# First attention and feed-forward of a two-layer block as one stage

## The chip, the cores and the metric

The kernel runs on one core of a Trainium2 chip. Such a core has TensorE (PE, matrix products and transposes), VectorE (DVE), ScalarE (ACT), GpSimd (POOL) and SyncE (SP, which here only issues DMAs). Each works through its own list of instructions in order, and they wait for each other by semaphores. The metric is the time of one execution on the device, in microseconds; lower is better.

## The reference

Four residual blocks on 2048 tokens of 256 values (8 sequences of 256), each followed by a layer norm. The change touches the first two:

```python
x = _layernorm(x + _L0_attn_ref(x, w_qkv, w_out, ln_scale, ln_bias))
x = _layernorm(x + _L0_ffn_ref(x, w_gate, w_up, w_down))
...
# attention, 16 heads of 16 values: q and k are rotated (rope), then normalised per head
a = jnp.einsum('bhnd,bhmd->bhnm', q, k) ** 4     # causal: the upper triangle is 0
out = einsum('bhnm,bhmd->bhnd', a / sum(a), v) @ w_out
# feed-forward, 1024 hidden values
return (silu(x @ w_gate.T) * (x @ w_up.T)) @ w_down.T
```

Then come a second attention (32 heads of 8, softmax with a bias) and a mixture of 8 experts with a shared one.

## The kernel before

Every matrix product with weights is done with operands split into a rounded high part and a rest: `product3` adds high x high, high x low and low x high, lines 415 to 417, so each product is three matmuls. ACT or POOL writes the high part, DVE or POOL the low one.

The kernel has four stages in order: first attention (`phase0`), first feed-forward (`feed_forward`), second attention (`phase2`) and the experts (`moe`). Every engine's code calls one function for each.

**First attention.** Eight batches of 256 tokens. A batch is worked off in eight slots, `p` = 0 to 7, each with two heads. In a slot PE does `scores` (lines 693 and 694, into banks 2 (p mod 2) and the next), ACT squares them out of PSUM (line 1258), POOL sets the upper triangle to zero (`affine_select`, line 2132, two instructions a slot), and the second squaring (`quartic`) falls to DVE in even slots (line 1661) and to ACT in odd ones (line 1241). In every second slot PE mixes four heads with v (`mix`, line 714). Between these each slot has a share of what the next batches need: `x_turn` (transpose x), `qk`, `v`, rotation and norm of the heads on DVE (`rope_half`, `centre`, `variance`, `normalised`, `times_scale`, `plus_bias`, `lo_parts`), their high parts on ACT (`hi_parts`, line 1228), `heads` (transposes, line 639), and of what the last batch needs: `c_turn`, `ct_turn`, `project`, `add`, `statistics`, `norm`. The tables `PE0` and `ACT0` say in which slot each stands. The one square root of a batch on ACT is `deviation` (line 1219). Middle batches run in a loop (`passes`).

POOL also splits the weights of the feed-forward: one unit of 128 x 768 a batch, in four pieces of 192 columns, a cast (line 2089) and a subtraction (line 2094) after each mask pair.

A finished batch is stored to `x1` in memory.

**First feed-forward.** Four passes of 512 tokens, each read back from `x1`. A pass has eight tiles of 128 hidden values: `gate_up` (12 matmuls of 512 columns, gate and up in two banks, two pairs of banks in turn), `silu` on ACT (line 1360), `product` on DVE (line 1814), `hidden_hi` on ACT, `hidden_lo` on DVE (line 1819), and two tiles later `down` (12 matmuls of 256 columns). The last pass has the start of the second attention between its tiles (`start_attention`).

## Time and profile before

| | |
|---|---|
| Median of three runs | 1083.01 us (1082.18 to 1087.15) |
| Profiled execution, its own time | 1081.15 us |
| Its span, first to last instruction | 1079.4 us |
| Mean granted PE clock | 0.945 |
| PE busy | 895.1 us, 83% |
| DVE busy | 701.5 us, 65% |
| ACT busy | 663.7 us, 61% |
| POOL busy | 292.6 us, 27% |

Busy shares are means over all stages. Matmuls are pipelined: a matmul's own length includes its way through the array, and the spacing of two starts is what one more costs. The clock is a share of full speed.

### The profile page before, as it was taken

The numbers are of one execution on the slowest core, as the hardware profiler recorded it, in microseconds if no ns is written. First come the engines' busy times: TensorE is split into PE (matmuls) and PEld (weight loads), VectorE is DVE, ScalarE is ACT, GpSimd is POOL, SyncE is SP. The second block draws the span as 40 slices with busy tenths as digits, with TensorE's granted clock in tenths as the row PEclk, the third lists the DMA queues.
The fourth block names the chain that finished last, engine by engine and source line by source line (L and its number), as shares of the span: only waits on it lengthen the run. The fifth ranks groups of instructions, "written<-read, shape, count | busy, mean of one in ns | idle before, by whom it ended". The sixth has DMA issues, their size and how long they took to land.

```text
span 1079.4 us, 21316 instructions
## 1 busy us (share of the span) xinstructions
PE 895.1 (83%) x6816; PEld 708.0 (66%) x6816; DVE 701.5 (65%) x2026; ACT 663.7 (61%) x1398; POOL 292.6 (27%) x417
## 2 busy tenths in 40 slices
PE   3577676766999998888888989898988899799993
PEld 2355555554888887566665656565655688698882
DVE  4767888883444455767788877888787654255445
ACT  2466667676232233888888878888888533256643
POOL 0255555455010110200202020202020226534436
PEclk9778989898899999999999999999999999999997
DMA  3001100112233310200101010111010402234443
GB/s 104 1 26 44 41 20 26 44 35 75 77 110 118 108 50 1 70 2 25 38 23 36 23 36 23 36 23 50 1 52 2 130 21 81 92 99 114 113 154 124
DMA packets 64868, 60.67 MB, mean 56 GB/s; under 512 B 18113, under 2 KB 60353, under 8 KB 64802
## 3 DMA queue, kind: packets, MB, share of 16 engines
q1 hardware_dynamic: 61394, 50.48, 16.0%
q0 software_dynamic: 3408, 9.34, 2.6%
q8 instruction: 38, 0.62, 0.3%
q14 instruction: 28, 0.23, 0.1%
HBM read 37.05 MB, written 22.75 MB: 55 GB/s over the span
## 4 chain that ended last, share of the span: by engine, by line
PE 50%; ACT 15%; DVE 14%; issue 11%; POOL 5%; DMA 2%; SPq 1%; DVEq 0%; ACTq 0%; POOLq 0%
PE ps L415 10%; PE ps L416 9%; PE ps L417 9%; ACT G L1310 6%; PE ps L821 6%; PE ps L639 4%; PE ps L838 3%; POOL xs L2216 3%; DVE G L1731 3%; PE ps L809 2%; ACT G L1320 2%; PE ps L714 2%; DVE RT L1652 1%; ACT G L1258 1%; ACT RT L1199 1%
## 5 line engine op out<-in xcount | busy, mean ns | idle before, releaser
L1310 ACT ACTIVATE G<-G,small 128x256 f32<-128x256 f32 x512 | 230.9, 506 | 54.7 <-DVE small L1731 53.3
L1731 DVE CUSTOM_DVE_ANT_0 G<-ps,nb 128x256 f32<-128x256 f32 x512 | 191.1, 419 | 74.9 <-PE ps L809 74.2
L821 PE MATMUL ps<-ident,G 128*128 128x128 f32 x1024 | 161.6, 288 | 39.9 <-ACT G L1310 38.0
L821 PEld LDWEIGHTS ps<-ident,G 128*128 128x128 f32 x1024 | 112.5, 143 | 76.3 <-issue 29.1
L2110 POOL TENSOR_SCALAR small<-small 128x2 f32<-128x2 f32 (+1 forms) x20 | 8.0, 400 | 461.7 <-DVE small L1535 461.7
L1320 ACT COPY G<-ps 128x512 f32<-128x512 f32 x192 | 111.3, 580 | 14.5 <-PE ps L821 14.1
L2132 POOL TENSOR_SCALAR_AFFINE_SELECT G<-G 128x256 f32<-128x256 f32 x128 | 75.7, 614 | 121.9 <-ACT G L1258 121.5
L639 PE MATMUL ps<-ident,RT 128*128 128x128 f32 x512 | 74.6, 293 | 20.2 <-DVE RT L1652 19.4
L415 PE MATMUL ps<-WU 128*128 128x512 f32 (+1 forms) x256 | 87.9, 343 | 1.5 <-DVE WU L1804 1.4
L416 PE MATMUL ps<-WU 128*128 128x512 f32 (+1 forms) x256 | 86.9, 340 | 0.0
L417 PE MATMUL ps<-WU 128*128 128x512 f32 (+1 forms) x256 | 86.6, 338 | 0.0
L639 PEld LDWEIGHTS ps<-ident,RT 128*128 128x128 f32 x512 | 61.3, 150 | 29.1 <-DVE RT L1652 15.7
L1360 ACT ACTIVATE G<-ps 128x512 f32<-128x512 f32 x32 | 19.1, 598 | 96.8 <-PE ps L417 96.8
L838 PE MATMUL ps<-G 128*32 128x256 f32 x1024 | 71.2, 397 | 0.8 <-ACT G L1320 0.8
L1814 DVE TENSOR_TENSOR G<-ps,G 128x512 f32<-128x512 f32 x32 | 22.1, 691 | 76.1 <-PE ps L417 76.1
L809 PE MATMUL ps<-RT 32*128 32x256 f32 x512 | 64.8, 331 | 6.8 <-DVE small L1731 2.8
L1258 ACT ACTIVATE G<-ps 128x768 f32<-128x768 f32 x64 | 52.1, 815 | 29.4 <-PE ps L694 28.2
L714 PE MATMUL ps<-ring,G 128*32 128x128 f32 (+1 forms) x512 | 32.5, 378 | 43.1 <-ACT G L1191 24.3
L809 PEld LDWEIGHTS ps<-RT 32*128 32x128 f32 x512 | 38.3, 184 | 42.0 <-issue 26.5
L415 PE MATMUL ps<-AW,RT 128*128 128x512 f32 (+1 forms) x128 | 54.2, 423 | 10.7 <-DVE nb L1707 4.4
L2094 POOL TENSOR_TENSOR WU<-wraw,WU 128x192 f32 (+4 forms) x56 | 57.4, 1024 | 1.9
L2251 POOL DMA_INDIRECT yy<-G x39 | 37.4, 959 | 65.8 <-ACT G L1454 65.8
(231 smaller groups left out, 2248.1 us busy)
## 6 DMA issues: line engine op xcount, KB each, us to landing
xs<-G SPq DMA_DIRECT2D x8, 645.0 KB, 7.1
G<-x SPq DMA_DIRECT2D x10, 512.0 KB, 4.5
G<-xs SPq DMA_DIRECT2D x39, 128.0 KB
G<-in_x SPq DMA_DIRECT2D x16, 256.0 KB, 2.9
G<-x SPq DMA_DIRECT2D x16, 256.0 KB, 3.3
wu_rows<-yy SPq DMA_DIRECT2D x8, 512.0 KB, 7.8
x<-G SPq DMA_DIRECT2D x15, 256.0 KB, 2.2
wraw<-in_wu SPq DMA_DIRECT2D x9, 384.0 KB, 3.6
```

Source lines behind the costliest of these rows:

```text
L415: pe.matmul(o, lh, rh, start=start, stop=False, skip_group_check=True)
L416: pe.matmul(o, lh, rl, start=False, stop=False, skip_group_check=True)
L417: return pe.matmul(o, ll, rh, start=False, stop=stop, skip_group_check=True)
L639: m = pe.transpose(ps[:, bank, S * g + P * t:S * g + P * (t + 1)], w[:, t, 2 * n + g, :], ident[:])
L809: m = pe.matmul(ps[:, SCORE_BANKS[n % 3], S * t:S * (t + 1)], QT[r, g, P * t:P * (t + 1)], KTT[r, g, :], start=True, stop=True, tile_posit ...
L821: m = pe.transpose(ps[:, 2 + h % 2, S * kt + P * t:S * kt + P * (t + 1)], prob(h)[:, t, P * kt:P * (kt + 1)], ident[:])
L838: m = pe.matmul(ps[32 * j:32 * j + 32, MIX_BANK, S * (quad % 2):S * (quad % 2 + 1)], vp[:, kt, at:at + 32], probT(h)[:, kt, :], start=kt = ...
L1258: act.square(U(p), ps[:, b:b + 2, 0:384]).then_inc(squared, 1)
L1310: m = act.activation(prob(h)[:, t, :], prob(h)[:, t, :], ACT.Exp, scale=-1.0, bias=mneg[:, k:k + 1])
L1320: act.copy(probT(h), halves(2 + h % 2)).then_inc(probT_act, 1)
L1731: m = dve.tensor_tensor_reduce(prob(h)[:, t, :], ps[:, SCORE_BANKS[h % 3], S * t:S * (t + 1)], nbv[:, t, :], 1.0, -FMIN, ALU.add, ALU.min, ...
L2132: m = pool.affine_select(out=u, in_=u, compare_op=ALU.is_ge, fill=0.0, base=0, pattern=[[0, 2], [1, P]], channel_multiplier=-1)
```

## The change

Both stages become one function, `first_layer`. The first attention keeps its eight batches of eight slots, now written out without a loop. From the third batch on (`LAG1` = 2) each slot also has one tile of the feed-forward, for the 256 tokens of the batch two before: PE does `gate_up(m)` behind `scores` and `down(m - 1)` at the slot's end. 47 of the 64 tiles stand in slots; the other 17 come behind the last slot, together with the end of the last batch and the start of the second attention. A tile has 256 tokens, gate and up side by side in one bank; in the slots this is always bank 6, behind them banks 0 and 1 in turn. The scores have one pair of banks (0, 1), and in the first two batches bank 6 and 7 in odd slots. Work is placed anew: the tables `PE0` and `ACT0` are gone, and functions `dense` and `slot` say what stands where.

The rows of a batch stay in SBUF (`X1`) from the attention's norm to the feed-forward's; `x1` in memory is gone. POOL splits all eight weight units of 768 columns ahead of its first mask (`raw_part`); SP loads six of them into free room at the start and the last two as room comes free. The filler rows for `xs` are stored during the second to fifth batch, and the four parts of the second attention's weights are split late in the first attention and behind it.

```diff
 TILES1 = F1 // P
+LAG1 = 2
+IN_BATCHES = 6
+RAW1 = 6
+AW2_ORDER = (0, 2, 1, 3)
+FILLS = 8
 TILES3 = -(-(NEXP * IE + SI) // P)
...
+        def score_bank(i, p):
+
+            return 6 if i < LAG1 and p % 2 else 0
+
+        def gate_bank(m):
+
+            return 6 if m < TILES1 * IN_BATCHES else m % 2
+
+        def z_bank(b):
+
+            return 2 if b == iterations[1] - 1 else 7
+
+        MIX0 = 2
...
+            def raw_load(j):
+                sp.dma_start(raw_tile[j % RAW1], wu1[j]).then_inc(raw_loaded[j // 4], 16)
...
+            for j in range(2):
+                raw_load(j)
+            sp.wait_ge(xt_turned[0], 1)
+            sp.dma_start(xt_in_a, rows(x, 1, 2)).then_inc(xt_loaded[0], 16)
+            for j in range(2, RAW1):
+                raw_load(j)
+            sp.wait_ge(diag_ready, 1)
...
+                if i == 0:
+                    for j in range(RAW1, TILES1):
+                        sp.wait_ge(split_w, j - RAW1 + 1)
+                        raw_load(j)
...
+                def gate_up(m):
+
+                    b, j = divmod(m, TILES1)
+                    if b == 0:
+                        pe.wait_ge(split_w, j + 1)
+                    pe.wait_ge(xt_ready[1], b + 1)
+                    if m >= TILES1 * IN_BATCHES + 2:
+                        pe.wait_ge(prod_ready[1], m - 1)
+                    elif m >= TILES1 * IN_BATCHES:
+                        pe.wait_ge(squared, pairs * n)
+                    elif m:
+                        pe.wait_ge(prod_ready[1], m)
+                    for w in range(2):
+                        for k in range(KT):
+                            c = slice((w * KT + k) * P, (w * KT + k + 1) * P)
+                            o = product3(pe, ps[:, gate_bank(m), S * w:S * (w + 1)], WU[:, j, 0, c], WU[:, j, 1, c],
+                                         XT_1[b % 2][0][:, k, :], XT_1[b % 2][1][:, k, :], k == 0, k == KT - 1)
+                    o.then_inc(gate_ready[1], 1)
+
+                def down(m):
+
+                    b, j = divmod(m, TILES1)
+                    pe.wait_ge(hid_ready[1], m + 1)
+                    if j == 0 and b == n - 1:
+                        pe.wait_ge(o_copied[0], 2 * n)
+                    elif j == 0 and b:
+                        pe.wait_ge(ffn_step, 3 * b - 2)
+                    for t in range(2):
+                        tok = slice(P * t, P * (t + 1))
+                        o = product3(pe, ps[:, z_bank(b), E * t:E * (t + 1)], HT_1[:, m % 2, 0, tok], HT_1[:, m % 2, 1, tok],
+                                     WU[:, j, 0, 2 * KT * P:UNIT], WU[:, j, 1, 2 * KT * P:UNIT], j == 0 and t == 0, j == TILES1 - 1)
+                    o.then_inc(down_done[1], 1)
+
...
+                def x1_turn(b):
+
+                    pe.wait_ge(xo_ready, NORMS[0] + b + 1)
+                    for k in range(KT):
+                        for t in range(2):
+                            m = pe.transpose(ps[:, 3, S * k + P * t:S * k + P * (t + 1)], X1[b % 2][:, t, P * k:P * (k + 1)], ident[:])
+                    m.then_inc(xt_turned[1], 1)
...
+                def slot(i, p):
+
+                    m = pairs * (i - LAG1) + p - 1
+                    scores(i, p)
+                    if m >= 0:
+                        gate_up(m)
+                    if p % 2 and (p > 1 or i):
+                        mix(i if p > 1 else i - 1, (p // 2 - 1) % 4)
+                    dense(i, p)
+                    if m >= 1:
+                        down(m - 1)
...
+                def silu(m):
+
+                    act.wait_ge(gate_ready[1], m + 1)
+                    if m >= 2:
+                        act.wait_ge(prod_ready[1], m - 1)
+                    act.activation(sg[:, m % 2, :], ps[:, gate_bank(m), 0:S], ACT.Silu).then_inc(silu_ready[1], 1)
...
+                def slot(i, p):
+
+                    m = H0 // 2 * (i - LAG1) + p - 1
+                    square(i, p)
+                    if p == 2 and i < n - 1:
+                        centred_squares(i + 1)
+                    if m >= 1:
+                        hidden_hi(m - 1)
+                    if p % 2 == 0 and (p or i):
+                        quartic(i, p - 1, not i)
+                    if p not in (4, 5) and m >= 0:
+                        silu(m)
+                    dense(i, p)
+                    if p in (4, 5) and m >= 0:
+                        silu(m)
+                    if p == 3 and i < n - 1:
+                        deviation(i + 1)
...
+                def product(m):
+
+                    dve.wait_ge(silu_ready[1], m + 1)
+                    if m >= 2:
+                        dve.wait_ge(hid_ready[1], m - 1)
+                    dve.tensor_tensor(hf[:, m % 2, :], ps[:, gate_bank(m), S:2 * S], sg[:, m % 2, :], ALU.mult
+                                      ).then_inc(prod_ready[1], 1)
...
+                def slot(i, p):
+
+                    m = H0 // 2 * (i - LAG1) + p - 1
+                    left = n - 1 - i
+                    if p % 2:
+                        quartic(i, p - 1, not i)
+                    if m >= 1:
+                        hidden_lo(m - 1)
+                    if p == 0 and left:
                         rope_half(i + 1, 1)
-                    quartic(i, 0, first)
-                    if left:
+                    if p == 1 and left:
+                        rotated(i + 1)
+                    if p == 2 and i > LAG1:
+                        x1_added(i - LAG1 - 1)
+                        x1_statistics(i - LAG1 - 1)
+                    if p == 4 and left:
+                        times_scale(i + 1)
+                    if p == 5:
+                        if left > 1:
+                            x_lo(0, i + 2)
+                        if i:
+                            context_lo(0, i - 1)
+                    if p == 6 and left:
+                        lo_parts(i + 1, 1)
+                    if p == 7 and i:
+                        norm(0, i - 1, 2, xr_a, X1[(i - 1) % 2])
+                    if m >= 0:
+                        product(m)
+                    if p == 0 and i >= LAG1:
+                        x1_lo(i - LAG1)
+                    if p == 1 and left:
                         centre(i + 1)
-                    quartic(i, 2, first)
-                    if left:
+                    if p == 2 and left:
                         variance(i + 1)
-                    if not first:
-                        context(0, i - 1, 0, D0)
-                    if left:
-                        normalised(i + 1)
-                        times_scale(i + 1)
-                        plus_bias(i + 1)
-                    if not first:
-                        context(0, i - 1, 1, D0)
-                    quartic(i, 4, first)
-                    if not first:
-                        context_lo(0, i - 1)
-                    if left > 1:
-                        x_lo(0, i + 2)
-                    if left:
-                        lo_parts(i + 1)
-                    if not first:
+                    if p == 3:
+                        if i:
+                            for c in range(2):
+                                context(0, i - 1, c, D0)
+                        if left:
+                            normalised(i + 1)
+                    if p == 4:
+                        if left:
+                            plus_bias(i + 1)
+                        if i > LAG1:
+                            x1_norm(i - LAG1 - 1)
+                    if p == 5 and left:
+                        lo_parts(i + 1, 0)
+                    if p == 6 and i:
                         dve.wait_ge(y_ready[0], i)
                         add(0, i - 1, 2, xr_a, (B_Y[0],))
                         statistics(0, i - 1, 2, xr_a)
-                    quartic(i, 6, first)
...
+            def raw_part(j):
+
+                pool.wait_ge(raw_loaded[j // 4], 64)
+                split_hi_part(j, WU[:, j, 0, :], raw_tile[j % RAW1])
+                split_lo_part(j, WU[:, j, 1, :], WU[:, j, 0, :], raw_tile[j % RAW1])
```

Three places in the order of instructions, one row each for an instruction or a run of equal ones.

ACT before, in a middle batch from the staging of v (1182) on; 1258 squares scores, 1241 is `quartic`, 1203 and 1228 make high parts, 1246 copies the mixed heads:

```order
L1182 COPY G<-ps 128x512
L1258 ACTIVATE G<-ps 128x768
L1241 ACTIVATE ring<-G 128x768
L1203 CAST WU<-ps 128x512
L1258 ACTIVATE G<-ps 128x768
L1228 CAST RT<-G 128x32x16 x4
L1258 ACTIVATE G<-ps 128x768
```

ACT of the change, the same place (slots 3 to 5; 1246 is now `deviation`, 1285 the squares, 1304 `hidden_hi`, 1297 `silu`, 1204, 1260 and 1200 copies of transposes, 1255 the casts of `head_hi_parts`):

```order
L1246 ACT_TABLE_LOAD
L1246 ACTIVATE small<-small 128x64
L1285 ACTIVATE G<-ps 128x768
L1304 CAST WU<-wu_rows 128x256
L1268 ACTIVATE ring<-G 128x768
L1204 CAST RT<-ps 128x512
L1260 CAST RT<-ps 128x512
L1200 CAST RT<-ps 128x512
L1297 ACT_TABLE_LOAD
L1297 ACTIVATE wu_rows<-ps 128x256
L1285 ACTIVATE G<-ps 128x768
L1304 CAST WU<-wu_rows 128x256
```

Two table loads and two instructions of the tile have come in between; `silu` of slot 4 stands behind three copies.

POOL before, at the start, from the memset of the ones to the first masks (2132) and split pieces (2089, 2094):

```order
L2086 MEMSET G 128x640
L2132 AFFINE_SELECT G<-G 128x2x128 x2
L2089 CAST WU<-wraw 128x192
L2132 AFFINE_SELECT G<-G 128x2x128 x2
L2094 TENSOR_TENSOR WU<-wraw,WU 128x192
```

POOL of the change at the same place, the end of the eight pairs of splits (2172, 2177), then the filler (2238, 2239) and the first masks (2228):

```order
L2172 CAST WU<-wu_rows 128x768
L2177 TENSOR_TENSOR WU<-wu_rows,WU 128x768
L2238 MEMSET G 128x5x257
L2239 IOTA G 128x5
L2228 AFFINE_SELECT G<-G 128x2x128 x30
```

The splits have moved from between the masks to before them.

DVE of the change in slots 4 and 5 of a merged batch (1743 `hidden_lo`, 1703 `times_scale`, 1737 `product`, 1707 `plus_bias`, 1641 `x1_norm`, 1725 `quartic`, 1589 `x_lo`, 1604 `context_lo`, 1716 `lo_parts`):

```order
L1743 TENSOR_TENSOR WU<-wu_rows,WU 128x256
L1703 TENSOR_TENSOR G<-G,lnt 128x1024
L1737 TENSOR_TENSOR wu_rows<-ps,wu_rows 128x256
L1707 TENSOR_TENSOR G<-G,lnt 128x1024
L1641 TENSOR_SCALAR G<-G,small 128x256 x2
L1725 TENSOR_TENSOR ring<-G 128x768
L1743 TENSOR_TENSOR WU<-wu_rows,WU 128x256
L1589 TENSOR_TENSOR RT<-ps,RT 128x512
L1604 TENSOR_TENSOR WU<-ps,WU 128x512
L1737 TENSOR_TENSOR wu_rows<-ps,wu_rows 128x256
L1716 TENSOR_TENSOR RT<-G,RT 128x32x16 x2
```

A `product` in each slot stands between pieces of the head norm, and what follows it waits with it.

## Rows read from the trace of the kernel before

**Rows 1.** The page, part 1: busy time, share and instructions by engine.
```profile
PE 895.1 (83%) x6816; PEld 708.0 (66%) x6816; DVE 701.5 (65%) x2026; ACT 663.7 (61%) x1398; POOL 292.6 (27%) x417
```

**Rows 2.** Busy time by stretch: PE, PEld, DVE, ACT, POOL, granted clock, DMA.
```profile
42.20:103.10 60.90, 41.91 (x321) 31.66 (x320) 43.54 (x58) 38.07 (x61) 31.82 (x50) 0.80 0.08 21
103.10:219.40 116.30, 82.67 (x723) 63.98 (x722) 93.86 (x140) 79.67 (x128) 63.08 (x104) 0.91 0.12 38
...
270.30:425.50 155.20, 149.68 (x861) 131.41 (x860) 69.47 (x138) 47.47 (x87) 13.66 (x18) 0.98 0.26 81
```

**Rows 3.** Order of time on PE (start, length, instruction), first scores of batches.
```profile
39.63 0.79 PE L415 MATMUL ps<-AW,RT 128*128 128x512 f32 x1
...
42.16 0.39 PE L693 MATMUL ps<-RT 64*128 64x256 f32 x2
...
103.13 0.39 PE L693 MATMUL ps<-RT 64*128 64x256 f32 x2
...
219.39 0.39 PE L693 MATMUL ps<-RT 64*128 64x256 f32 x2
...
422.39 1.04 PE L639 MATMUL ps<-ident,RT 128*128 128x128 f32 x8
425.53 0.50 PE L809 MATMUL ps<-RT 32*128 32x256 f32 x4 [2.10 <-DVE G L1523]
```

**Rows 4.** Order of time on PE: spacing in a batch, and in the feed-forward.
```profile
207.02 0.39 PE L693 MATMUL ps<-RT 64*128 64x256 f32 x2
...
207.44 0.86 PE L714 MATMUL ps<-ring,G 128*32 128x256 f32 x16
...
215.67 0.86 PE L714 MATMUL ps<-ring,G 128*32 128x256 f32 x16
216.46 1.09 PE L639 MATMUL ps<-ident,RT 128*128 128x128 f32 x8
...
291.14 0.40 PE L415 MATMUL ps<-WU 128*128 128x512 f32 x1
...
293.88 0.28 PE L415 MATMUL ps<-WU 128*128 128x256 f32 x1
...
295.32 0.40 PE L415 MATMUL ps<-WU 128*128 128x512 f32 x1
```

**Rows 5.** DVE groups by form, 103.1 to 219.4 us: busy, mean ns, idle before.
```profile
L1560 DVE TENSOR_TENSOR G<-ps,small 128x256 f32<-128x256 f32 x8 | 3.4, 424 | 0.3
...
L1564 DVE TENSOR_TENSOR WU<-ps,WU 128x512 fp32r<-128x512 f32 x4 | 2.7, 678 | 0.0
```

**Rows 6.** ACT: a 256-element group, and the order of time around a table load.
```profile
L1199 ACT ACTIVATE RT<-ps 128x256 fp32r<-128x256 f32 x8 | 2.4, 394 | 0.0
...
25.37 0.57 ACT L1173 CAST RT<-ps 128x512 fp32r<-128x512 f32 x1
25.96 1.28 ACT L1219 ACT_TABLE_LOAD   x1
27.25 0.35 ACT L1219 ACTIVATE small<-small 128x64 f32<-128x64 f32 x1
...
208.84 2.20 ACT L1228 CAST RT<-G 128x512 fp32r<-128x512 f32 x4
```

**Rows 7.** POOL groups by form, its first mask, and GB/s in slices of 1.25 us.
```profile
L2132 POOL TENSOR_SCALAR_AFFINE_SELECT G<-G 128x256 f32<-128x256 f32 x128 | 75.7, 614 | 121.9 <-ACT G L1258 121.5 <-POOL WU L2094 0.3
...
L2094 POOL TENSOR_TENSOR WU<-wraw,WU 128x192 f32 x20 | 16.7, 834 | 0.0
L2094 POOL TENSOR_TENSOR WU<-wraw,WU 128x704 fp32r<-128x704 f32 x8 | 13.4, 1681 | 0.6
...
L2089 POOL CAST WU<-wraw 128x704 fp32r<-128x704 f32 x8 | 6.2, 770 | 10.9 <-DMA wraw<-in_wu 10.9
...
43.63 0.77 POOL L2132 TENSOR_SCALAR_AFFINE_SELECT G<-G 128x256 f32<-128x256 f32 x2 [40.92 <-ACT G L1258]
...
GB/s 0 39 345 247 267 329 61 7 0 2 46 83 181 110 0 0 0 0 0 233 292 0 0 0 0 0 0 0 0 0 0 0 0 0 0 13 0 0 0 0
```

More of the change, by code:

```diff
@@ L784, in phase0 @@
                 heads(0, 0, 1)
-                pe.wait_ge(heads_q[0], 2)
-                qk(0, 1, 1)
-                passes(pe, n, one)
-                mix(n - 1, H0 // 4 - 1, False, 0)
-                for c in range(2):
-                    c_turn(0, n - 1, c, 4, True)
+                pe.wait_ge(bias_ready, 1)
+                pe.wait_ge(v_staged[0], 1)
+                for i in range(n):
+                    for p in range(pairs):
+                        slot(i, p)
+                last = TILES1 * IN_BATCHES
@@ L792, in phase2 @@
+                for k in range(2):
+                    down(last + 2 * TILES1 - 2 + k)
             def phase2():
[L794 to L795 removed]
+                pe.wait_ge(ffn_step, 3 * iterations[1] - 2)
+                pe.wait_ge(filled, 16 * FILLS)
                 n = iterations[2]
@@ L1690, in one @@
                         statistics(0, i - 1, 2, xr_a)
-                    quartic(i, 6, first)
-                    if not first:
-                        norm(0, i - 1, 2, xr_a, xo_a)
-                    if left > 1:
+                    if p == 7 and left > 1:
                         rope_half(i + 2, 0)
```

898 lines of the change are left out of this document (438 added, 460 removed).

## The prediction

> **What bounds the kernel now.** I read the page, then the busy time of the stages, then the order of time on TensorE (PE) at the starts of batches, then the costs by line. The page says PE is busy for 83% of the span [rows 1]. That is a mean over stages of two kinds [rows 2]. In the feed-forward stage (270.3 to 425.5 us) PE is busy for 149.7 of 155.2 us: it alone is the bound, and VectorE (DVE, 69.5 us) and ScalarE (ACT, 47.5 us) mostly wait for it. In the four middle batches of the first attention (103.1 to 219.4) nobody is full: PE 82.7, DVE 93.9, ACT 79.7, GpSimd (POOL) 63.1 us of 116.3. Four engines hand 16 heads from one to the next, and the time lies in the handing over. PE's granted clock says the same: 0.91 of full speed there, 0.80 in the first two batches, 0.98 in the feed-forward.
>
> So the two stages are unlike, and the merge puts PE work into PE's holes. The first scores start at 42.16, the third batch at 103.13, the seventh at 219.39, the second attention at 425.53 [rows 3]. A middle batch takes (219.39 - 103.13) / 4 = 29.06 us. The change touches only what lies before 425.53; there the sum is made. The feed-forward of 256 tokens costs 155.2 / 8 = 19.4 us of span today, so a merged batch breaks even at 48.5 us.
>
> **PE's part.** Twelve 512-column matmuls take 293.88 - 291.14 = 2.74 us and twelve of 256 columns 295.32 - 293.88 = 1.44 us [rows 4]: 0.228 and 0.120 each. A new tile is 12 + 6 matmuls of 256 columns, 18 x 0.12 = 2.16 us; an old one, for twice the tokens, is 4.18. Halving the tile costs PE only 64 x 0.07 = 4 us in all. Packed, the attention part of a batch is 8 scores x 0.42, 4 mixes x 0.79, 48 transposes x 0.11 (a group of eight is 1.09 with its tail, 0.87 without), 12 matmuls of 512 columns and 24 of 256: 3.4 + 3.2 + 5.2 + 2.7 + 2.9 = 17.4 us [rows 4]. With eight tiles (17.3) and one more set of transposes (0.4) a merged batch holds PE for 35.1 us.
>
> **The other engines.** DVE has 93.9 / 4 = 23.5 us a batch [rows 2], and gets sixteen 256-element operations at 0.42 (6.7), one subtraction and one addition of 512 elements at 0.68, and two rows each of statistics, their aggregation and the norm, about 2.1 at that price: together 33.7 us [rows 5]. ACT has 79.7 / 4 = 19.9, and gets sixteen operations at 0.39, a copy at 0.57, and something the diff does not show, table loads: Silu now stands between the Squares and the one Sqrt of a batch, so each batch switches tables twice, at 1.28 us [rows 6]. The changed program's list has 16 loads in place of 5. ACT: 29.3 us. POOL has 63.1 / 4 = 15.8, loses four pairs of split operations (the subtraction alone is 0.83 [rows 7]), and comes to about 11. So PE (35.1) and DVE (33.7) are both nearly full, and the queues, in order on four engines, decide.
>
> **A merged batch, slot by slot.** I walked one batch with these durations, each instruction starting when its engine and its inputs are there. PE's eight slots come out at 4.4, 5.3, 4.2, 5.2, 3.9, 6.1, 6.9 and 5.6 us, 41.5 in all. PE waits 6.4 of them: 1.0 in slot 1 (`gate_up` of a new batch behind `x1_turn`, `x1_hi` and `x1_lo`), 1.0 in slot 3 (`product` stands behind `x1_added` and `x1_statistics`), and 4.1 in slots 5 and 6. The last are one loop: there is one gate bank (6), so `gate_up(m+1)` waits for `product(m)`, and that for `silu(m)`. In slot 4 silu stands behind three copies and a table load; in slot 5 behind the four casts of `head_hi_parts`, 2.2 us [rows 6]. Late next is `lo_parts(1)` on DVE, queued behind that product, and with it `heads(i+1, 0)` on PE.
> The price in dispute is the table load. In the trace one runs from 25.96 to 27.24; the instruction before it ends at 25.94, the next starts at 27.25 [rows 6]. I take 1.28, as the walk does.
> The Trainium skill (ScalarE: Activation LUTs, section What ACT_TABLE_LOAD costs) gives 1283 ns and a drain of about 1380 ns more for every switch, and advises to do all work of one set before the next, which speaks against this change. By it, as an estimate, ten switches in five batches add up to 14 us; the row agrees with the 1283 and shows no drain.
> Such a walk is too short, as it has no handover time and always the full clock. For a batch of the new order without tiles it gives 27.8, where the old batch, of the same work, takes 29.06. I add 4%.
>
> **The sum.** Until the first scores: 42.2. The eight splits of 768 elements now stand on POOL ahead of all masks. From the 704-element pair, (0.77 + 1.68) x 768 / 704 = 2.67 us, 21.4 for eight [rows 7]. Four tiles must have landed first; SP can issue the fourth at about 14.5, once x is turned, and 1.6 MB at the 250 to 345 GB/s of this prologue's loads [rows 7] is there near 19. POOL is through at 40 to 43 and the filler follows (1.5): first mask at 42 to 45, against 43.63 now. If DVE slows the splits as it slows the masks (0.61 in the mean, 0.38 in the first pair), it is 50, 6 us late. The other way, `qk(0, 1, 1)`, on PE from 39.63 to the first scores [rows 3], goes behind them. Together I take 0, bounds -3 and +7.
> First two batches, without tiles: 61, as now.
> Six merged batches: the third has no x1 norm yet (40), three full ones (124.5), the seventh lacks what prepares a ninth (39.5), and the last prepares nothing, 28.6 on PE and about 31 with the gate-bank loop: 235, with 4% 244 us.
> The tail: 17 tiles x 2.16 = 36.7, and between them on PE the last batch's mix, turns and projection and the second attention's start, 10.3 by the unit prices above, and some 1 us for `x1_lo` at the eighth. It has two gate banks and is PE-bound: 48. From the last `down` to the second attention 3 us, as now (422.4 to 425.5 [rows 3]).
> 42.2 + 61 + 244 + 48 + 3 = 398 against 425.5: 27 us earlier. The second attention then starts with two norm rows less (about -1). The transfers of x1 to memory and back vanish; only their start (part of the 19.4) was on the path. The profiled execution took 1081.15 us (span 1079.4, 1.8 around it), the median of three is 1083.0; 28 less on the median's scale is 1055.
>
> **The rivals.**
> (a) This forecast, 1040 to 1068: 0.58.
> (b) The waits close up and PE is the bound, at 35 to 38 us a batch. For it: PE was busy for 96% of the feed-forward. Against: one gate bank, and DVE at 33.7. Six batches of 5 us less: 1025 (1015 to 1040). 0.12.
> (c) Handovers cost as much as today, where a batch holds 29.06 - 17.4 = 11.7 us beyond PE's work. Then a merged batch is 46.8 and four batches cost 3.6 us more each, the outer two as much: 1077 (1068 to 1084). 0.10.
> (d) Each table switch holds ACT for about the length of a second load: ten of them, 13 us, all on the loop: 1068. 0.05. This is the skill's drain; the one row so far speaks against it.
> (e) Slower: silu gates every slot. ACT must give `square` to the attention and `silu` to the gate bank in the same slot, and each waits for PE in turn. If that makes `product(m)` 1 us later than walked in each of 47 slots, a merged batch is 51 and the time 1102 (1084 to 1105). It decides from 27 / 47 = 0.57 us a slot, a batch of 47.8. For it: ACT is in order and has 29 us of work. Against: the hole is spread, and masks get quicker as the splits leave. 0.12.
> (f) What is won in the slots is lost in the prologue and the second attention's start, 1083: 0.03.
>
> **How the numbers follow.** Likeliest is (a): 1055. A change under 0.5%, 5.4 us, can hardly be told from none here. Faster: (a), (b), (d) and half of (c), 0.80; same: the rest of (c) and (f), 0.08; slower: (e), 0.12. The range leaves out the lower half of (b) and (e): 1024 to 1081; the forecast's own is 1040 to 1068.
>
> **What would show it.** The second attention's first scores near 398 us. Merged batches of 42 to 44 us from the third on, PE busy for over 80% of them at a clock over 0.95. The largest PE waits in slots 5 and 6, for `product` on DVE, with DVE waiting for silu. Eleven more table loads of 1.28 us with nothing idle behind them. The first mask between 41 and 50. A tail of 48 us with PE full. It is wrong if PE waits for `product` in every slot, if 256-column matmuls don't keep 0.12 us, or if the masks start past 50.

## The result, and the profile after

The changed kernel took 1075.45 us, the median of five runs (1071.86 to 1079.20), where the kernel before took 1084.01 (1082.18 to 1087.26) beside it: a ratio of 0.9913, 95% interval 0.989 to 0.9935. It is faster clear of noise, but by 9 us (0.9%) where 28 were forecast. The prediction of 1055 was 20 us too low.

The page of the kernel after, parts 1 and 5 (the latter's columns: busy us, mean ns of one, idle us before and what ended it):

```profile
PE 900.7 (84%) x7200; PEld 728.3 (68%) x7200; DVE 716.2 (67%) x2090; ACT 682.8 (64%) x1472; POOL 290.5 (27%) x377
...
L437 PE MATMUL ps<-WU 128*128 128x256 f32 x384 | 120.2, 313 | 36.4 <-DVE wu_rows L1737 24.9
L2228 POOL TENSOR_SCALAR_AFFINE_SELECT G<-G 128x256 f32<-128x256 f32 x128 | 79.8, 647 | 182.6 <-ACT G L1285 182.6
```

PE has less idle time, but 24.9 us of what is left stands before the first matmul of a feed-forward tile, ended by `product` (L1737). That is the loop which the walk had found. The masks (L2228) are slower than before, 647 ns against 614 [rows 7], though no split runs beside them any more.

Busy time by stretch, columns as in [rows 2]. Batches are counted from 0, so batch 2 is the first merged one; batches 3 to 5 are called steady, since they hold the same work. The rows shown are the prologue, batches 0 and 1 together, batch 2, batch 4, the tail (from the first `gate_up` behind the last slot to the second attention's first scores) and the rest of the program:

```profile
0.00:47.40 47.40, 16.60 (x60) 11.88 (x60) 28.72 (x31) 11.36 (x16) 30.00 (x29) 0.78 0.38 117
47.40:105.90 58.50, 41.94 (x323) 31.68 (x322) 41.02 (x55) 38.23 (x63) 23.01 (x34) 0.82 0.09 28
105.90:147.50 41.60, 34.40 (x305) 29.65 (x304) 30.04 (x50) 28.51 (x49) 11.69 (x18) 1.00 0.19 57
...
193.90:240.20 46.30, 40.26 (x332) 34.94 (x330) 32.96 (x61) 28.30 (x51) 12.41 (x20) 0.93 0.15 48
...
364.40:421.80 57.40, 51.49 (x406) 49.13 (x406) 29.52 (x75) 19.80 (x53) 7.29 (x11) 0.97 0.09 29
421.80:1072.20 650.40, 566.20 (x4528) 440.07 (x4528) 439.91 (x1605) 452.45 (x1052) 153.12 (x181) 0.97 0.19 56
```

Set beside the sum of the prediction:

| term | forecast | measured |
|---|---|---|
| first scores | 42.2 | 47.4 |
| batches 0 and 1 | 61 | 58.5 |
| six merged batches | 244 | 258.5 (41.6, 46.4, 46.3, 45.9, 44.2, 34.1) |
| tail and end | 51 | 57.4 |
| second attention's first scores | 398 | 421.8 |
| from there to the end | 1 less | 650.4, 3.5 less than the 653.9 of before |

So three terms were short: 5 us in the prologue, 14.5 in the merged batches, 6.5 in the tail, against 2.5 gained in the first two batches.

**The loop.** There is one gate bank, so `gate_up` waits for the last tile's `product`, that for silu, and silu for what stands ahead of it on ACT. First the order of time on ACT of the kernel after, then on PE, around slots 4, 5 and 6 of batch 4:

```profile
217.18 0.60 ACT L1200 CAST RT<-ps 128x512 fp32r<-128x512 f32 x1
217.80 1.28 ACT L1297 ACT_TABLE_LOAD   x1
219.09 0.38 ACT L1297 ACTIVATE wu_rows<-ps 128x256 f32<-128x256 f32 x1
219.37 0.81 ACT L1285 ACTIVATE G<-ps 128x768 f32<-128x768 f32 x1
...
224.73 0.59 ACT L1230 CAST WU<-ps 128x512 fp32r<-128x512 f32 x1 [4.26 <-PE ps L678]
225.21 2.17 ACT L1255 CAST RT<-G 128x512 fp32r<-128x512 f32 x4
227.29 0.38 ACT L1297 ACTIVATE wu_rows<-ps 128x256 f32<-128x256 f32 x1
```

```profile
220.14 0.35 PE L437 MATMUL ps<-WU 128*128 128x256 f32 x1 [2.00 <-DVE wu_rows L1737]
220.33 0.28 PE L438 MATMUL ps<-WU 128*128 128x256 f32 x1
220.45 0.28 PE L439 MATMUL ps<-WU 128*128 128x256 f32 x1
...
221.05 0.41 PE L438 MATMUL ps<-WU 128*128 128x256 f32 x1
221.27 0.42 PE L439 MATMUL ps<-WU 128*128 128x256 f32 x1
...
222.26 1.51 PE L728 MATMUL ps<-ring,G 128*32 128x256 f32 x16
223.70 0.99 PE L678 MATMUL ps<-ident,G 128*128 128x128 f32 x4
...
228.27 0.55 PE L437 MATMUL ps<-WU 128*128 128x256 f32 x1 [2.49 <-DVE wu_rows L1737]
228.62 0.41 PE L438 MATMUL ps<-WU 128*128 128x256 f32 x1
228.83 0.41 PE L439 MATMUL ps<-WU 128*128 128x256 f32 x1
```

PE idles 2.00 us in slot 5 and 2.49 in slot 6, each time for `product`, whose silu stands behind copies on ACT. In slot 6 ACT itself idles 4.26 us ahead of `context_hi` (L1230) with silu queued behind it. The walk had 4.1 us for the two; this step was right. Behind the table load the next instruction starts at once (217.80 + 1.28 = 219.08, and 219.09), so there is no drain.

What the walk had not: the square of slot 5 (219.37) is behind the load too, so the score banks come free later as well. And the lower clock: a mix takes 1.51 us here, 0.86 before [rows 4], and 256-column matmuls follow each other every 0.21 us (228.62, 228.83), not every 0.12. PE had idled before: behind the wait of 2.00 us the first matmuls still come every 0.12 us (220.33, 220.45), and from 221.05 on every 0.22; behind the wait of 2.49 us they are slow from the start. That is the 1.2 GHz level; the row of this batch has 0.93 of the full clock.

**The prologue.** Order of time on DVE of the kernel after (the chain from L1683 to L1707 centres and normalises the heads, L1716 makes their low parts), and then two rows of POOL beside it:

```profile
20.86 1.79 DVE L1683 TENSOR_TENSOR G<-G 128x1024 f32<-128x1024 f32 x1
22.68 1.22 DVE L1684 TENSOR_REDUCE small<-G 128x64 f32<-128x1024 f32 x1
...
29.49 2.21 DVE L1699 TENSOR_TENSOR G<-G,small 128x1024 f32<-128x1024 f32 x1
31.74 1.73 DVE L1703 TENSOR_TENSOR G<-G,lnt 128x1024 f32<-128x1024 f32 x1
33.50 2.71 DVE L1707 TENSOR_TENSOR G<-G,lnt 128x1024 f32<-128x1024 f32 x1
37.48 6.51 DVE L1716 TENSOR_TENSOR RT<-G,RT 128x512 fp32r<-128x512 f32 x4 [1.27 <-ACT RT L1255]
```

```profile
32.47 2.66 POOL L2177 TENSOR_TENSOR WU<-wu_rows,WU 128x768 fp32r<-128x768 f32 x1
35.07 1.81 POOL L2172 CAST WU<-wu_rows 128x768 fp32r<-128x768 f32 x1
```

POOL is done in time (the filler ends at 46.9, the first square starts at 47.96). But both engines are slowed, and DVE's chain leads to the first scores. In the kernel before, where no split ran beside it, the chain's ends were:

```profile
20.64 1.23 DVE L1622 TENSOR_TENSOR G<-G 128x1024 f32<-128x1024 f32 x1
...
33.49 2.50 DVE L1652 TENSOR_TENSOR RT<-G,RT 128x512 fp32r<-128x512 f32 x4 [1.27 <-ACT RT L1228]
```

So the chain took 15.4 us before (20.64 to 35.99) and 23.1 after (20.86 to 43.99). From its end to the first square it was 6.7 us before and is 4.0 after. E1 shows that the splits are the cause of the first.

### The profile page after: what moved, and what is told of

Its sections match the earlier page's. It is cut to its first block, busy times and chain, and to the rows that moved or that the text cites. A ratio compares the mean times of both kernels' runs of the same rounds, so it can differ in the third digit from the quotient of the medians.

```text
span 1072.2 us, 21733 instructions
## 1 busy us (share of the span) xinstructions
PE 900.7 (84%) x7200; PEld 728.3 (68%) x7200; DVE 716.2 (67%) x2090; ACT 682.8 (64%) x1472; POOL 290.5 (27%) x377
## 4 chain that ended last, share of the span: by engine, by line
PE 49%; DVE 18%; ACT 14%; issue 11%; POOL 4%; DMA 2%; SPq 0%; DVEq 0%; ACTq 0%; POOLq 0%
PE ps L437 9%; PE ps L438 8%; PE ps L439 8%; ACT G L1401 6%; PE ps L937 5%; PE ps L655 5%; PE ps L954 3%; POOL xs L2317 3%; DVE G L1876 3%; PE ps L925 2%; PE ps L728 2%; ACT G L1411 2%; PE ps L670 1%; ACT RT L1226 1%; PE ps L1117 1%
## 5 line engine op out<-in xcount | busy, mean ns | idle before, releaser
L437 PE MATMUL ps<-WU 128*128 128x256 f32 x384 | 120.2, 313 | 36.4 <-DVE wu_rows L1737 24.9
L2228 POOL TENSOR_SCALAR_AFFINE_SELECT G<-G 128x256 f32<-128x256 f32 x128 | 79.8, 647 | 182.6 <-ACT G L1285 182.6
L438 PE MATMUL ps<-WU 128*128 128x256 f32 x384 | 111.6, 291 | 0.0
L439 PE MATMUL ps<-WU 128*128 128x256 f32 x384 | 111.5, 290 | 0.0
L437 PEld LDWEIGHTS ps<-WU 128*128 128x128 f32 x384 | 75.9, 198 | 44.0 <-issue 28.8
L2193 POOL TENSOR_SCALAR small<-small 128x2 f32<-128x2 f32 x16 | 7.1, 443 | 354.6 <-DVE small L1573 354.6
L438 PEld LDWEIGHTS ps<-WU 128*128 128x128 f32 x384 | 76.2, 198 | 0.2
L439 PEld LDWEIGHTS ps<-WU 128*128 128x128 f32 x384 | 76.3, 199 | 0.0
L1297 ACT ACTIVATE wu_rows<-ps 128x256 f32<-128x256 f32 x64 | 24.4, 381 | 58.7 <-PE ps L439 58.6
L1737 DVE TENSOR_TENSOR wu_rows<-ps,wu_rows 128x256 f32<-128x256 f32 x64 | 26.7, 417 | 48.8 <-ACT wu_rows L1297 38.7
L1204 ACT CAST RT<-ps 128x512 fp32r<-128x512 f32 x64 | 36.9, 576 | 33.6 <-PE ps L655 33.6
```

The lines of the kernel that those rows point to most:

```text
L437: pe.matmul(o, lh, rh, start=start, stop=False, skip_group_check=True)
L438: pe.matmul(o, lh, rl, start=False, stop=False, skip_group_check=True)
L439: return pe.matmul(o, ll, rh, start=False, stop=stop, skip_group_check=True)
L2228: m = pool.affine_select(out=u, in_=u, compare_op=ALU.is_ge, fill=0.0, base=0, pattern=[[0, 2], [1, P]], channel_multiplier=-1)
```

## The experiments

Chips differ in pace: the program from the second attention on, which no experiment touches, took 650 us in the profile above, 649 and 655 in those of C2 and E11, and 668 to 675 in those of C and E1 to E10. So each timed ratio is to the kernel before on the same chip, and the stages are compared by landmarks that the trace gives within the stage: the first square on ACT of a batch, and the first instruction of the second attention on DVE ("second attention" below; 426.2 before, 422.5 after). The tail is counted here from the last square to there. C and C2 are the changed kernel again. Nine of these profiles (all but E1, E4, E6, E8 and E9) have the changed kernel's prologue and first two batches unchanged: their first squares lie between 47.5 and 48.7, and batches 0 and 1 together take 57.6 to 59.9 us. Smaller differences than these are not read.

| kernel | first square | steady batches 3 to 5 | tail | second attention | ratio (95%) |
|---|---|---|---|---|---|
| changed | 48.0 | 46.4, 46.1, 46.1 | 62.0 | 422.5 | 0.9913 (0.989 to 0.9935) |
| E1 splits spread | 38.8 | 43.9, 44.7, 44.6 | 62.0 | 415.8 | 0.9944 (0.9912 to 0.9975) |
| E2 silu early in 4 | 48.6 | 42.1, 43.1, 42.8 | 61.8 | 408.0 | 0.9834 (0.9785 to 0.9883) |
| E3 silu early in 4, 5 | 47.7 | 41.1, 40.8, 40.7 | 61.9 | 397.3 | 0.9758 (0.972 to 0.9796) |
| E4 no table switch | 49.2 | 43.7, 43.4, 42.1 | 61.9 | 411.7 | 0.9826 (0.9783 to 0.9869) |
| C changed, again | 47.8 | 46.4, 46.1, 46.0 | 62.0 | 424.3 | 0.989 (0.9846 to 0.9933) |
| E5 keep the clock | 48.2 | 43.9, 43.5, 43.5 | 62.0 | 417.1 | 0.992 (0.9892 to 0.9948) |
| E6 = E3, splits late | 41.4 | 41.1, 40.7, 40.7 | 60.5 | 390.9 | 0.9668 (0.9633 to 0.9702) |
| E7 = E3, tail order | 47.5 | 41.1, 40.7, 40.7 | 57.8 | 394.9 | 0.9719 (0.9686 to 0.9752) |
| E8 = E6 and E7 | 39.3 | 41.1, 40.8, 40.8 | 57.8 | 387.3 | 0.965 (0.9621 to 0.968) |
| E9 = E8, no switch | 40.4 | 40.9, 40.6, 40.6 | 57.8 | 388.0 | 0.967 (0.9639 to 0.9701) |
| E10 clock, batches 3 to 6 | 47.8 | 43.9, 43.5, 43.5 | 62.0 | 415.0 | 0.9889 (0.9855 to 0.9924) |
| C2 changed, beside E11 | 48.7 | 43.9, 44.9, 44.6 | 62.0 | 419.3 | 0.9955 (0.9932 to 0.9977) |
| E11 = E10, beside C2 | 48.5 | 43.9, 43.5, 43.5 | 62.0 | 416.7 | 0.9884 (0.9848 to 0.992) |

### First set: the prologue, silu's place, the table

E1, the splits out of the prologue, half of one per slot (POOL):

```diff
-            for j in range(TILES1):
-                raw_part(j)
...
                     masks(i, p)
+                    if i < 2:
+                        raw_half(8 * i + p)
```

> GpSimd's sixteen instructions that split the feed-forward's weights leave the prologue and run one per slot behind the masks of the first two batches. Theory (in the prologue GpSimd's splits slow VectorE's elementwise chain, which sets the first scores): VectorE's L1699, L1707 and L1716 are back at about 1.2, 1.2 and 0.6 each, first scores at 39 to 42 instead of 47.4; batches 0 and 1 take 0 to 3 us longer than 58.5 because the masks now share GpSimd with the splits; the whole is 1068 to 1073. Rival (the prologue is late because its loads or the bias through device memory are): VectorE's chain may be faster, but the first scores stay at 46 to 48 and the time at 1075 or above.

The prologue gave back all that was asked of it and more: L1699, L1703 and L1707 took 1.2 each and the four of L1716 2.5 us together, where the kernel after took 2.2, 1.7, 2.7 and 6.5. The chain from L1683 on took 15.4 us again (18.91 to 34.27), 7.8 less than in the kernel after; the first square came 9.2 us earlier, since the chain also started 1.9 us earlier. The chain's ends in E1:

```profile
18.91 1.23 DVE L1683 TENSOR_TENSOR G<-G 128x1024 f32<-128x1024 f32 x1
...
31.77 2.50 DVE L1716 TENSOR_TENSOR RT<-G,RT 128x512 fp32r<-128x512 f32 x4 [1.27 <-ACT RT L1255]
```

The rival falls. But the first two batches took 31.6 and 36.1 where they had taken 27.9 and 30.5: +9.3 us, all of it lost again, and more than the 0 to 3 expected. So the forecast of the whole missed too: 0.9944, which is 1078 beside 1084, and not 1068 to 1073. Order of time on DVE and POOL of E1, batch 0:

```profile
45.76 1.83 DVE L1689 SCALAR_TENSOR_TENSOR G<-small,G 128x1024 f32<-128x1024 f32 x1
51.96 2.39 DVE L1699 TENSOR_TENSOR G<-G,small 128x1024 f32<-128x1024 f32 x1
...
59.06 4.51 DVE L1716 TENSOR_TENSOR RT<-G,RT 128x512 fp32r<-128x512 f32 x4
```

```profile
59.13 2.27 POOL L2177 TENSOR_TENSOR WU<-wu_rows,WU 128x768 fp32r<-128x768 f32 x1
61.36 1.67 POOL L2236 TENSOR_SCALAR_AFFINE_SELECT G<-G 128x256 f32<-128x256 f32 x2
```

The same three take 1.23, 1.23 and 2.50 in batch 0 of the kernel after, where no split runs beside them: 3.8 us together, as much as the batch got longer (3.7). In batch 1 they give 2.4 of its 5.7 us; the rest was not followed. That DVE's chain sets the pace of these batches too is the likely reading; E6 bears it out. The 7 us by which the second attention came earlier stem from the steady batches' clock, which C2 shows to come and go.

E2 and E3, silu ahead of ACT's copies in slot 4 (E2), in slots 4 and 5 (E3):

```diff
-                    if p not in (4, 5) and m >= 0:
+                    if m >= 0:                        # E2: p != 5
                         silu(m)
                     dense(i, p)
-                    if p in (4, 5) and m >= 0:
-                        silu(m)
```

> In slot 4 ScalarE takes silu (and with it the table load) ahead of its copies of the turned heads and of the next x; slot 5 as in the changed kernel. Theory (the six merged batches are long because gate_up of slots 5 and 6 waits for product, which waits for silu behind copies, while the gates have one bank): the wait of 2.0 us in slot 5 goes, a steady batch falls from 46.2 to 44.0 to 45.0, the whole by 8 to 12 us, to 1064 to 1068. Rival (the work after the slot is bound by what VectorE and TensorE's own order carry, and the wait only moves to slot 6 or to the heads' copies): batch 45.8 to 46.4, time within 3 us of 1075.

> silu ahead of the copies in slots 4 and 5 both. Theory: both waits of the loop (2.0 and 2.5 us a batch) shrink, a steady batch at 42 to 43.5, the whole 1056 to 1064. Rival (in slot 5 the context's and the heads' copies then come later, and heads of slot 6 and the projection wait for them, so the time comes back in slots 6 and 7): slot 5 and 6 shorter, 6 and 7 longer by the same, batch no shorter than with slot 4 alone, 1064 to 1075.

Both theories held, with shorter batches than expected: 42.7 us a steady batch with E2 and 40.9 with E3. The eight slots of batch 4 (square to square) show where: 4.55, 5.43, 4.94, 4.75, 5.20, 8.19, 7.14, 5.91 in the kernel after, 4.56, 5.44, 4.92, 4.76, 4.87, 5.27, 7.36, 5.92 in E2, and 4.55, 5.44, 4.93, 4.75, 4.87, 4.99, 5.31, 5.92 in E3. Nothing came back in slots 6 and 7, so E3's rival falls. Busy time of E3's batch 5, columns as above, and the largest of PE's waits in its batch 4 (us in total, times, longest):

```profile
226.00:267.00 41.00, 37.92 (x333) 32.81 (x332) 32.62 (x61) 28.17 (x52) 12.41 (x20) 1.00 0.05 17
```

```profile
PE ps L437 <- DVE WU L1728: 0.8, 1, 0.8
PE ps L437 <- DVE wu_rows L1735: 0.7, 3, 0.3
```

The wait for `product` is 0.7 us in place of 4.7 in the kernel after, PE is busy for 92%, and the clock is full. One reordering on ACT is worth 25 us of the stage in the profiles. In time it is 1.3 to 2.0% of the whole, 14 to 21 us, by the three ratios of the changed kernel (0.989, 0.9913 and 0.9955); E3 was not timed beside it.

E4, no table switch:

```diff
-                    act.activation(hrs, hvar, ACT.Sqrt, scale=1.0 / D0, bias=eps_col)
+                    act.activation(hrs, hvar, ACT.Identity, scale=1.0 / D0, bias=eps_col)
```

> The square root of the heads' deviation is replaced by Identity with the same scale and bias (this leaves the square root out of the computation), so that ScalarE keeps one table through the whole stage. Theory (a table load costs its 1.28 us on ScalarE and matters only where silu gates the loop, once a batch): six merged batches shorter by 0.7 to 1.3 us each, whole 1067 to 1071. Rival (each load also drains or delays what is behind it by another microsecond or more): shorter by 2 us a batch and more, 1060 or below. Second rival (loads stand in ScalarE's idle time): within 2 us of 1075.

Slot 4 went from 5.20 to 4.02, nearly the load's 1.28; slot 5 from 6.68 (where the clock was up) to 6.45. That is 1.4 us a batch, just above the theory's 0.7 to 1.3. The batches fell by 2.7 to 3.9, which is the rival's figure, but the surplus is the lower clock, which came in fewer slots: slot 6 was 7.3 twice and 6.1 once, never 8.6. The rival's further microsecond behind a load is not in the rows, and the second rival falls. The time (0.9826, or 1065 beside 1084) lies between the theory's and the rival's and decides nothing.

### Second set: the clock, a better place for the splits, the tail

> The changed kernel itself, beside the other runs of this call on the same chip, since a chip's own pace moves all times. Both theories: 0.988 to 0.994 of the kernel before, the six merged batches at about 46 each.

C has 0.989, and steady batches of 46.4, 46.1 and 46.0. Not all six are near 46: the third batch took 43.2 us, the seventh 44.2.

E5, extra matmuls in PE's two waits:

```diff
                     scores(i, p)
+                    if i > LAG1 and p in (5, 6):
+                        for _ in range(p - 1):
+                            pe.matmul(ps[0:64, 7, 0:S], ident[0:64, 64:P], WU[0:64, 0, 0, 0:S].bitcast(F32),
+                                      start=False, stop=False, skip_group_check=True)
```

> In the merged batches TensorE runs 4 extra matmuls in slot 5 and 5 in slot 6 (256 columns in float32, zeros added to the feed-forward's sums), where it waits 2.0 and 2.5 us for the gates. The waits stay, TensorE is not idle in them. Theory (half of what the merged batches lost against the walk is the clock at its lower level behind those waits, 2.5 us a batch): granted clock 1.00 in the steady batches, slots 5 and 6 together 12.5 to 13.5 instead of 15.3, batch 43.5 to 44.5, the whole 1060 to 1067 on the pace of the first measurement, 0.975 to 0.983 of before. Rival (the slow pieces are contention, or the dummies delay the gates): batches 46 or longer, ratio 0.99 or above.

Busy time of batch 4 of E5, columns as above, and one of its fillings in the order of time on PE:

```profile
193.00:239.00 46.00, 44.25 (x368) 37.16 (x367) 34.16 (x63) 29.85 (x54) 13.07 (x22) 1.00 0.18 56
```

```profile
217.50 1.94 PE L833 MATMUL ps<-WU,ident 64*64 64x256 f32 x8
219.57 0.35 PE L437 MATMUL ps<-WU 128*128 128x256 f32 x1
```

`gate_up` still comes 2 us late, but PE is busy up to it, the clock stays at 1.00, and slots 5 and 6 take 12.7 us (6.68 and 6.07) where the kernel after takes 15.3. So 2.55 us a batch are the clock's lower level, behind waits of 4.5, and the rival falls in the trace. In batch 7, where PE hardly waits, the fillings cost 2.9 us. The timed runs didn't follow: 0.992, in the rival's band and not in the theory's, which is why E10 came.

E6, on E3: one tile split in the prologue, the others where DVE's chain isn't the pace:

```diff
-            for j in range(TILES1):
-                raw_part(j)
+            raw_part(0)
...
+            WHEN = {(0, 6): (2,), (0, 7): (3,), (1, 0): (4,), (1, 6): (5,), (1, 7): (6, 7), (2, 0): (8, 9),
+                    (2, 1): (10, 11), (2, 2): (12,), (2, 3): (13,), (2, 4): (14,), (2, 5): (15,)}
```

> On the version with silu early in slots 4 and 5: one tile is split in the prologue, three and a half in slots 6, 7 and 0 of the first two batches, where VectorE waits for TensorE, the rest in slots 0 to 5 of the third batch. Theory (a split costs time only where VectorE's chain through memory sets the pace): first scores at 38 to 41, batches 0 and 1 at 57 to 60, the third batch 39 to 41, the whole 5 to 9 us below the version with early silu, 0.968 to 0.972 of before. Rival (wherever the splits go they cost what they save, as they did spread evenly): within 2 us of it, 0.974 to 0.978.

Held: first square 41.4, batches 0 and 1 57.7 together (57.7 in E3 too), the third 40.4 (38.9 in E3), the second attention 6.4 us earlier, and a ratio of 0.9668, just below the forecast band. Three tiles and not three and a half stood in the first two batches, as `WHEN` shows. The same instructions in E6, in order of time on DVE; POOL has ended its one split at 21.7:

```profile
31.88 1.22 DVE L1705 TENSOR_TENSOR G<-G,lnt 128x1024 f32<-128x1024 f32 x1
...
34.38 2.50 DVE L1714 TENSOR_TENSOR RT<-G,RT 128x512 fp32r<-128x512 f32 x4 [1.27 <-ACT RT L1255]
```

E7, on E3, the tail's order (ACT; DVE the same with `hidden_lo` and `x1_lo`):

```diff
                 x1_hi(n - LAG1)
+                hidden_hi(last - 1)
                 outputs(n - 1, 1)
                 for k in range(2 * TILES1):
-                    if k == 8:
-                        x1_hi(n - 1)
                     silu(last + k)
-                    hidden_hi(last + k - 1)
+                    if k:
+                        hidden_hi(last + k - 1)
+                    if k == 7:
+                        x1_hi(n - 1)
```

> On the version with silu early in slots 4 and 5: at the tail's start the hidden row's halves are taken ahead of the outputs' copy and of the next product, and the last batch's rows are split into halves at k = 7, ahead of the second attention's head parts. Theory (the tail's two waits of 1.3 and 1.8 us and the lower clock behind the second are its excess over the forecast): tail from the last square to the second attention's first scores at 57 to 59 instead of 61.9, ratio 0.971 to 0.974. Rival (the tail's excess is TensorE's own work, 51.5 us busy where 47.6 were forecast): 61 to 62, ratio 0.976.

The tail fell from 61.9 to 57.8. Its busy time from the last square on, first in E3, then in E7:

```profile
335.41:397.27 61.86, 55.32 (x444) 52.12 (x445) 32.55 (x84) 21.84 (x56) 9.54 (x15) 0.97 0.09 27
```

```profile
337.11:394.93 57.82, 53.67 (x444) 50.67 (x445) 32.87 (x84) 21.96 (x56) 9.56 (x15) 1.00 0.09 29
```

4.0 us were order: the wait at the start, the wait for `x1_lo`, and the clock behind it. The rival has the rest: PE works 53.7 of 57.8 us at full clock. Counted as in the table of terms, from the first `gate_up` behind the slots, E7's tail is 53.3 us:

```profile
340.97:394.28 53.31, 49.76 (x406) 47.61 (x406) 29.84 (x75) 19.97 (x53) 7.31 (x11) 1.00 0.10 31
```

### Third set: together, the table again, and the clock beside the changed kernel

> silu early in slots 4 and 5, the splits late, and the tail's new order together. Theory (the three shortfalls are separate stretches of the program and add up): first square at 41.4, third batch 40.4, steady batches 40.7, tail 57.8 or less, so the second attention's first scores at 387 to 389, and 0.962 to 0.966 of the kernel before. Rival (part of what one gives is waited for again elsewhere, the tail's turn of rows above all): 391 or later, 0.967 and above.

Held in the trace: 387.3. The three add up: 25.2 us (E3), 6.4 (E6) and 3.6 more. Of these 3.6, only 2.6 lie in the tail, which was 1.4 us shorter in E6 already; its first square came 2.0 us earlier than in E6 with the same splits, which none of the three orders explains, and the first two batches gave 0.8 back. In time it is 0.965, the best of all, but not told apart from E6's 0.967 by the intervals. On its chip 1063.5 us stand against 1102.6 before.

> The same with the heads' square root replaced by Identity (which leaves the square root out of the computation), so no table is loaded in the stage. Theory (a load costs its 1.28 us on ScalarE, and on the loop only in slot 4, where the square of the next slot stands behind it): slot 4 at 4.0 instead of 4.9, a steady batch at 39.8 to 40.0, the whole 4 to 7 us less. Rival (once TensorE is busy for over nine tenths of a batch the loads are hidden): batch 40.5 to 40.7, ratio equal within 0.002.

The theory fell. Slot 4 took 4.02 as forecast, but slot 5 then 5.64 in place of 4.98, a batch 0.2 us less, and the time no less (0.967). With silu early and PE busy for 92% the loads are hidden, where they cost 1.4 us a batch in E4. That the copies which they delay would wait anyway is argued, not shown.

E10 is E5 with `LAG1 < i < n - 1` in its condition, so it differs from E5 in batch 7 alone. The expectation below is wrong on the third batch (batch 2): E5 had no fillings there either. That batch took 44.3 us in E5, and as much in E10 and C2, behind unfilled waits and with slots 5 and 6 at 15.3 to 15.4: it is the lower clock, which the profile of the kernel after, at 41.7, happened to miss.

> The changed kernel with the extra matmuls in the waits of slots 5 and 6 of the four steady batches alone, not in those of the third and the last batch, where they had cost 1 and 3 us. Theory (the clock's lower level behind the waits costs 2.5 us a batch): steady batches 43.5, first scores of the second attention at 413 to 415, and the timed runs 0.979 to 0.984 of before. Rival (what the extra work keeps of the clock here is paid back by a lower clock in the rest of the program): batches 43.5 in the profile all the same, timed runs at 0.987 to 0.992, with a mean granted clock no higher than the changed kernel's.

The profile gave the 43.5 and 415.0, 9 us earlier than C; the timed runs stood at 0.9889, in the rival's band and above the theory's 0.984. With C on another chip, and single times of one kernel 7 to 11 us apart, this did not decide.

> The changed kernel as the control. If the lower clock behind the waits stands in every execution, slots 5 and 6 take 15.3 us together in each steady batch here too (third profile), and its timed runs lie 8 us or more above those with the extra matmuls. If it comes and goes, some steady batches take 12.7 here.

> The same extra matmuls in the four steady batches. Theory (the clock costs 2.5 us a batch in time, too): steady batches 43.5, 0.990 to 0.993 of the changed kernel beside it. Rival (paid back elsewhere): steady batches 43.5, and 0.997 to 1.003 of the changed kernel beside it.

Side by side the medians are 1072.65 and 1078.45: 0.9946, and the intervals to the kernel before don't touch (0.9848 to 0.992, 0.9932 to 0.9977). Of 72 pairs of a run of each, E11's is the shorter in 67. The ratio lies between the bands of the theory (0.990 to 0.993) and of the rival (0.997 to 1.003). The clock does cost time, 5.8 us of the 10 that four batches of 2.55 would make, and it isn't all paid back: the mean granted clock of a whole run is 0.953 in E11 and 0.945 in C2. C2's own profile says in part why less. Its batches took 43.9, 44.9 and 44.6; slot 5 was 6.68, 8.04 and 6.68, slot 6 6.06, 6.06 and 7.09. The work is the same in every execution, and PE's waits for `product` are too (4.7 us a batch in C2 as in the kernel after), but the lower level comes behind some of them only, in some executions behind all. What decides that is open; the waits of 2 to 2.5 us are what invites it, as it came in none of the filled batches and in none of E3's. Two cautions: C2's profile is of the fastest of its twelve runs, so the others may have had more of the lower level; and behind the stage the profile of E11 took 654.5 us, C2's 649.3. Whether part of the gain is paid back there, one profile of each can't tell.

## Why the prediction was wrong in size

Right were the direction and the mechanism: PE's holes took the feed-forward's work, each merged batch stayed under the 48.5 of break-even, and the two large waits stood in slots 5 and 6 for `product` behind silu. Of the signs of being wrong that it named, one came: 256-column matmuls don't keep 0.12 us but take 0.21 behind the waits. The clock of the merged batches was 0.93 where over 0.95 was forecast. The step that failed is the 4% on the walk, which stood for the handovers and the clock together, and did not hold the lower clock behind the new waits. Step by step:

- **Prologue, 0 taken, 5.2 measured.** The bounds of -3 and +7 held, but by two errors of opposite sign. The failed sentence is "If DVE slows the splits": it has the direction wrong for the path. POOL was through at 45.7 and its masks weren't waited for; the splits slowed DVE's chain (L1707 from 1.22 to 2.71), which cost 7.8 us of the path. 2.7 came back between the chain's end and the first square; that is the forecast's -3 (`qk(0, 1, 1)` behind the scores), though no run tests it alone. E1 and E6 have the first square 9.2 and 6.3 us earlier than the kernel that each changes. The sum priced the splits as POOL's time alone.
- **First two batches, 61 taken, 58.5 measured**: here POOL's pieces of the splits are gone. That this is the same contention with the other sign is argued, not shown, and part of the 2.5 us is within the spread of 57.6 to 59.9.
- **Merged batches, 244 taken, 258.5 measured, the largest miss.** The 4% turned the walk of 41.5 into 43.2; a steady batch took 46.1. The walk's waits were right (4.1 against 4.5). With the clock kept up (E5, E10) the batch takes 43.5, so the 4% nearly paid for what the walk itself lacked, 2.0 us; what stood in no term is the clock behind the new waits, 2.55. In batches 3 to 6 together it is 10.2 of the 14.5 us (kernel after less E10). Of the rest, 1.9 are in the last batch (34.1 against 31 with 4%). That the third batch hit its forecast, 41.6, is luck too: the clock stayed up in this profile, and the same batch took 43.2 in C and 44.3 in C2. Slot by slot the walk was shortest in slot 4 (3.9 walked, 5.2 measured), where the square of the next slot stands behind the load and silu as well; but its slots are PE's and the measured ones go from square to square, so this assignment is rough. A margin taken from a stage at a clock of 0.91 can't hold the drop that the new waits bring themselves.
- **The loop's price.** I booked 4.1 us for it. Taking it away (E3) gave 5.3: 2.7 of waits (43.5 with the clock kept up, 40.8 in E3) and 2.6 of clock.
- **Tail, 51 taken, 57.4 measured.** PE's work was put at 47 us; in E7, at full clock, PE is busy for 49.8 us of 53.3. So 2.3 us more than the forecast of 51 are PE's own, and 4.1 were waits with the clock behind them, which E7 removed.
- **Table loads.** 1.28 each and no drain: right, and rival (d) falls with it, on the rows of the kernel after (217.80 and 1.28, next at 219.09); E4's slots agree. The trace has ten more than before (15 against 5), where eleven were forecast. That they cost only 0.2 us a batch once silu stands early (E9) was not foreseen.
- **The rivals.** The time lies in the range of (c), 1068 to 1084, and the batch near its 46.8, but its reason, handovers as costly as before, isn't what E3 shows: the same handovers give 40.8 us when silu stands earlier. (b) did not come, and its 35 to 38 us a batch are not reached by E3 either, where PE alone is busy for 37.9 of 41.0 us and the forecast had it at 35.1. (e) did not come; silu gated two slots in eight.
- **After the stage, 1 less taken, 3.5 measured.** This was not followed up. The same part of the program takes 649 and 655 us in C2 and E11 on one chip, so 3.5 is within what single profiles differ by.
- **Masks.** "Masks get quicker" was wrong: 647 ns against 614 [rows 7].

That E3 reaches the forecast of 398 for the second attention, at 397.3, is luck: its batches are shorter than forecast, its prologue and tail longer.

## What to carry to other kernels

When a walk shows a loop through one buffer (gates, silu, product, gates), look first at what its small instruction stands behind in its own queue: moving silu ahead of the copies in two slots was worth more than the whole merge (1.3 to 2.0% against 0.5 to 1.1%). Price a wait of PE with the clock behind it, here up to 2.55 us a batch behind waits of 2.0 and 2.5. Work that is moved to a free engine is not free: POOL's splits cost the path where DVE's operations with two SBUF inputs were on it.

## What was unexpected of the hardware

POOL's splits and DVE slow each other, but not in every operation. A DVE operation with two inputs in SBUF and 1024 elements takes 1.22 us alone and 1.46 to 2.71 beside POOL's splits; a POOL cast of 768 elements 0.82 alone (at 18.05) and up to 1.82 beside DVE. On DVE, what has one input in SBUF keeps its time beside a split: the reduction of 1024 elements (L1684) 1.22 us, and the subtraction of PSUM and SBUF (L1589) 0.68, as in E6 with POOL silent. ACT's four casts do too (2.18 and 2.17). And the granted clock differs from one execution of the same work to the next: six timed runs of C stood at 0.936 to 0.946 and 1097.5 to 1086.0 us, those with the higher clock being the shorter.
